# The last three steps of a tiled transformer kernel written in another order

## The reference

```
x = x + fake_quant(layernorm(x)) @ fake_quant(ctx)     # ctx: 1024 x 1024 for each sequence
x = x + attention(layernorm(x))                        # 32 heads of 32, one k and v for all, causal, alibi, @ Wo
x = x + (xf * in_scale @ sign(W).T) * out_scale + bias # xf = layernorm(x); scales = softmax(router) @ tables
```

## Time and profile before

| | |
|---|---|
| timed runs | 408.24, 407.40, 408.12 us; median 408.12 |
| profiled execution | 407.38 us, of which the profile's span is 405.6 |
| PE busy over the span | 89% |
| DVE, ACT, POOL busy over the span | 77%, 63%, 33% |
| mean granted clock of PE | 0.982 of full (2.4 GHz) |

### The profile page before, as it was taken

How to read it: one execution, slowest core, us unless ns; L and a number is a source line. 1 busy time by engine, 2 the same in 40 slices (tenths; PEclk the granted TensorE clock), 3 DMA queues, 4 the chain that set the end, 5 groups by cost and what they waited for, 6 DMA issues and landing times.

```text
span 405.6 us, 10034 instructions
## 1 busy us (share of the span) xinstructions
PE 362.7 (89%) x4162; PEld 233.9 (58%) x4162; DVE 312.1 (77%) x592; ACT 253.8 (63%) x306; POOL 133.5 (33%) x148
## 2 busy tenths in 40 slices
PE   0438977999789999999999999999999999999996
PEld 0113943874444874578557855696559655974444
DVE  6888798999846788679876997589858975496353
ACT  3857985867787877783887388648865741334021
POOL 5320043426321226312541246124612371026041
PEclk9957999999999999999999999999999999999999
DMA  7999999399999499857867587748665000100002
GB/s 303 410 373 408 409 405 391 114 322 412 311 367 347 190 288 404 302 178 196 298 229 240 147 269 263 228 153 294 225 244 131 10 2 6 50 2 0 2 1 105
DMA packets 30243, 91.56 MB, mean 226 GB/s; under 512 B 8112, under 2 KB 8496, under 8 KB 30192
## 3 DMA queue, kind: packets, MB, share of 16 engines
q1 hardware_dynamic: 28320, 84.42, 58.5%
q10 hardware_dynamic: 1872, 6.40, 4.2%
HBM read 85.05 MB, written 4.19 MB: 220 GB/s over the span
## 4 chain that ended last, share of the span: by engine, by line
PE 60%; DVE 15%; DMA 9%; ACT 7%; SPq 4%; issue 3%; POOL 0%; DVEq 0%; ACTq 0%; POOLq 0%
DMA ring<-ctx 9%; PE R L1603 9%; PE T L1426 6%; PE R L1371 5%; PE R L1372 5%; PE R L1373 5%; PE C L1407 4%; ACT b L583 4%; PE R L1462 4%; PE R L1465 3%; PE R L1464 3%; PE T L1507 3%; SPq L371 2%; PE R L1491 2%; PE R L1378 1%
## 5 line engine op out<-in xcount | busy, mean ns | idle before, releaser
L583 ACT ACTIVATE b<-ring,quant,qpar 128x2048 uint8<-128x2048 f32 x61 | 126.4, 2093 | 14.3 <-DMA ring<-ctx 8.2
L1462 PE MATMUL R<-T_hi,Wqkv_hi 128*128 128x128 f16 x448 | 77.9, 220 | 0.0
L1465 PE MATMUL R<-T_hi,Wqkv_lo 128*128 128x128 f16 x448 | 77.7, 219 | 0.0
L1464 PE MATMUL R<-T_lo,Wqkv_hi 128*128 128x128 f16 x448 | 77.7, 219 | 0.0
L1407 PE MATMUL C<-b,aT 128*64 128x512 f16 x256 | 35.7, 411 | 12.9 <-ACT b L583 6.3
L485 POOL TENSOR_TENSOR Pr<-Pr,mx 128x512 f32<-128x512 f32 x32 | 35.4, 1118 | 30.5 <-DVE mx L1069 30.5
L334 POOL TENSOR_TENSOR Pr<-Pr,mx 128x512 f32<-128x512 f32 x20 | 20.7, 1044 | 74.7 <-DVE mx L1063 74.7
L1462 PEld LDWEIGHTS R<-T_hi,Wqkv_hi 128*128 128x128 f16 x448 | 43.9, 98 | 2.0
L1464 PEld LDWEIGHTS R<-T_lo,Wqkv_hi 128*128 128x128 f16 x448 | 43.9, 98 | 0.2
L1465 PEld LDWEIGHTS R<-T_hi,Wqkv_lo 128*128 128x128 f16 x448 | 43.8, 98 | 0.0
L1371 PE MATMUL R<-Wo,attT_hi 128*128 128x512 f16 x112 | 42.5, 379 | 0.6 <-DVE attT_lo L1081 0.5
(11 more groups left out here) (172 smaller groups left out, 845.4 us busy)
## 6 DMA issues: line engine op xcount, KB each, us to landing
ring<-ctx SPq DMA_DIRECT2D x64, 1024.0 KB, 7.7
ring<-L_attn_Wo SPq DMA_DIRECT2D x4, 1024.0 KB, 9.3
ring<-L_ffn_weight SPq DMA_DIRECT2D x4, 1024.0 KB, 5.2
Wo<-L_attn_Wqkv SPq DMA_DIRECT2D x7, 544.0 KB, 15.2
X<-x ACTq DMA_DIRECT2D x6, 512.0 KB, 4.6
out<-X ACTq DMA_DIRECT2D x6, 512.0 KB, 6.2
X<-x SPq DMA_DIRECT2D x2, 512.0 KB, 11.5
sgn<-L_attn_Wqkv SPq DMA_DIRECT2D x1, 544.0 KB, 18.0
```

Of the source, the lines that this page charges most:

```text
L583: e.activation(b8[:, c % BRING, :], ring[:, slot, :], ACT.Identity, scale=qR2, bias=qZ2).then_inc(s_rf[slot], 1)
L1462: e.matmul(dst, hi, rows[0], start=k == 0 and g == 0, stop=False, skip_group_check=True)
L1464: e.matmul(dst, hi, rows[1], start=False, stop=False, skip_group_check=True)
L1465: last = e.matmul(dst, lo, rows[0], start=False, stop=k == KT - 1, skip_group_check=True)
```

## The change

`opening` is no longer called for step 7, nor `tail` for steps 8 and 9; one function `closing(s, last, end)` with Step(7), Step(8), Step(9) holds what the three did, and `burst` is called up to step 6. In it, with m = 6 and t = 7:

- PE: the context product of tile 7 is finished and its T1 and kv, query and scores come before the projection of tile 6; T1 stands between the two halves of tile 5's second FFN product, before PT of tile 6's second head half. The projection of tile 6 lies around the scores and PT of tile 7; T2 and router of tile 6 lie between the pieces of tile 7's projection. The FFN of tile 6 comes behind it: 16 matmuls ahead of tile 7's T2, 8 between T2 and the router, 8 between router and router transpose. `keep_clock(15)` and `keep_clock(6)` go; the 2 and 3 stay.
- DVE: x1(7) comes ahead of the second row sum of tile 6, norm1 right behind O's low part; the softmax of tile 7 and tile 6's x2, norm2 and router chain are put in the new order.
- POOL: the three softmax operations of tile 6, then inv_std(1, 7), then bias and sums of tile 5; with_bias(7) comes ahead of both sums of tile 6.
- Banks: projection of tile 6 goes to C, outscale of tile 6 to R 2:4, the second scores of tile 7 to R 2:4 (before R 0:2). The T banks' uses are listed in the new order. Some waits are replaced by those that the new banks ask for.

The core of the diff (PE's program, the T banks and POOL's):

```diff
+    m, t = TILES - 2, TILES - 1
+    uses += of(m, "PT00 PT01 O0") + of(t, "T10 T11") + of(m, "PT10 PT11") + of(t, "Tk") + of(m, "O1")
+    uses += of(t, "PT00 PT01 O0 PT10 PT11") + of(m, "T20 T21") + of(t, "O1")
+    uses += of(m, "rl rT is0 is1") + of(t, "T20 T21 rl rT is0 is1")
...
+            def closing(s, last, end):          # POOL
+                m, t = s.i - 1, s.i
+                subtract_max(e, m, 1, 1)
+                normalize(m, 1, 0)
+                normalize(m, 1, 1)
+                inv_std(1, t)
+                with_bias(m - 1)
+                total(m - 1, 0)
+                total(m - 1, 1)
...
+            def closing(s, last, end):          # DVE
+                m, t = s.i - 1, s.i
+                row_sum(m, 1, 0)
+                pt_lo(s, 0, 0)
+                pt_lo(s, 0, 1)
+                x1(s)
+                row_sum(m, 1, 1)
+                o_lo(s, 0)
+                norm1(s)
+                result(s, 0)
+                t1_lo(s, 0)
+                t1_lo(s, 1)
...
+            def closing(s, last, end):          # PE
+                context(s.i, 2)
+                ffn(s, 0, low)
+                pt(s, 0, 0)
+                pt(s, 0, 1)
+                context(s.i, 3)
+                ffn(s, 0, high)
+                outscale(s, 0)
+                outscale(s, 1)
+                pv(s, 0)
+                ffn(s, 1, low)
+                t1(s)
+                ffn(s, 1, high)
+                pt(s, 1, 0)
+                pt(s, 1, 1)
+                kv(s)
+                query(s, 0, low[:2])
+                tk(s)
+                query(s, 0, low[2:])
+                pv(s, 1)
+                query(s, 0, high)
+                query(s, 1, low[:2])
+                scores(s, 0)
+                query(s, 1, low[2:])
+                query(s, 1, high)
+                project(s, 0, low)
+                scores(s, 1)
+                project(s, 1, low)
+                pt(last, 0, 0)
+                pt(last, 0, 1)
+                project(s, 0, high)
+                pv(last, 0)
+                project(s, 1, high)
+                pt(last, 1, 0)
+                pt(last, 1, 1)
+                project(last, 0, low)
+                t2(s)
+                project(last, 1, low[:2])
+                pv(last, 1)
+                project(last, 1, low[2:])
+                router(s)
+                project(last, 0, high)
+                router_t(s)
+                project(last, 1, high[:1])
+                inscale(s, 0)
+                inscale(s, 1)
+                outscale(last, 0)
+                outscale(last, 1)
+                project(last, 1, high[1:])
+                ffn(last, 0, low)
+                ffn(last, 0, high)
+                t2(last)
+                ffn(last, 1, low)
+                router(last)
+                ffn(last, 1, high)
+                router_t(last)
+                keep_clock(2)
...
-                keep_clock(15)
...
-                keep_clock(6)
```

More of the change, by code:

```diff
@@ L99, in turns @@
     uses += of(0, "T20 T21 rl rT is0 is1")
-    for i in range(2, TILES + 1):
+    for i in range(2, TILES - 1):
         if i > 2:
             uses += of(i - 1, "PT00 PT01 O0 PT10 PT11 O1")
-        uses += of(i, "T10 T11 Tk") if i < TILES else []
-        uses += of(i - 1, "T20 T21 rl rT is0 is1")
+        uses += of(i, "T10 T11 Tk") + of(i - 1, "T20 T21 rl rT is0 is1")
+    m, t = TILES - 2, TILES - 1
+    uses += of(m, "PT00 PT01 O0") + of(t, "T10 T11") + of(m, "PT10 PT11") + of(t, "Tk") + of(m, "O1")
+    uses += of(t, "PT00 PT01 O0 PT10 PT11") + of(m, "T20 T21") + of(t, "O1")
+    uses += of(m, "rl rT is0 is1") + of(t, "T20 T21 rl rT is0 is1")
     return {use: n for n, use in enumerate(uses)}
@@ L119, in link, with run_steps @@
         self.e.wait_ge(self.sem, self.n)
-def run_steps(entry, step_0, step_1, opening, burst, tail):
+def run_steps(entry, step_0, step_1, opening, burst, closing):
     entry()
@@ L127, in run_steps @@
     burst(Step(2))
-    for i in range(3, TILES):
+    for i in range(3, TILES - 1):
         opening(Step(i))
         burst(Step(i))
-    tail(Step(TILES), Step(TILES + 1))
+    closing(Step(TILES - 1), Step(TILES), Step(TILES + 1))
 def at_least(e, sem, value):
@@ L327, in scores_to @@
         def scores_to(t, h):
-            return R[:, 2:4, :] if t < 2 and h == 1 else R[:, 0:2, :]
+            return R[:, 2:4, :] if t in (0, 1, TILES - 1) and h == 1 else R[:, 0:2, :]
         def subtract_max(e, t, h, b):
@@ L343, in project_to @@
         def project_to(m, n):
+            if m == TILES - 2:
+                return C[:, n, :]
             return C[:, 1 - n, :] if m == 0 else R[:, n, :]
@@ L353, in ffn_to, with outscale_to @@
             return C[:, n, :] if t == TILES - 2 else R[:, 2 + n, :]
+        def outscale_to(t):
+            return R[:, 2:4, :] if t == TILES - 2 else R[:, 0:2, :]
         last_sums = (R[:, 2, :], C[:, 0, 0:HALF // 2], C[:, 1, 0:HALF // 2])
@@ L543, in burst @@
                 normalize(s.i, 0, 1)
-            def tail(s, last):
-                t = TILES - 1
+            def closing(s, last, end):
[7 more added lines that the diff above has]
+                total(m - 1, 1)
+                subtract_max(e, t, 0, 1)
+                normalize(t, 0, 0)
+                normalize(t, 0, 1)
                 subtract_max(e, t, 1, 1)
@@ L549, in tail @@
                 normalize(t, 1, 1)
-                with_bias(t - 1)
-                total(t - 1, 0)
+                inv_std(2, m)
+                with_bias(m)
                 inv_std(2, t)
                 with_bias(t)
-                total(t - 1, 1)
+                total(m, 0)
+                total(m, 1)
                 x_t = X[t % XBUFS]
@@ L559, in tail @@
                     e.tensor_tensor(x_t[:, cols], x_t[:, cols], XL[:, cols], ALU.add).then_inc(s_y, 1)
-            run_steps(entry, step_0, step_1, opening, burst, tail)
+            run_steps(entry, step_0, step_1, opening, burst, closing)
         @block.scalar
@@ L612, in outscale_copy @@
                     e.wait_ge(s_y, t * 2)
-                e.activation(XL[:, :], R[:, 0:2, :].rearrange("p a n -> p (a n)"), ACT.Identity)\
+                e.activation(XL[:, :], outscale_to(t).rearrange("p a n -> p (a n)"), ACT.Identity)\
                     .then_inc(s_ose, 1)
@@ L858, in burst @@
                     conv(s.i + 1, 6)
-            def tail(s, last):
-                t = TILES - 1
-                exp(t, 1, 0)
+            def closing(s, last, end):
+                m, t = s.i - 1, s.i
+                conv(t, 7)
+                exp(m, 1, 0)
                 pt_hi(s, 0, 0)
                 pt_hi(s, 0, 1)
-                exp(t, 1, 1)
+                exp(m, 1, 1)
+                o_hi(s, 0)
                 outscale_copy(s)
-                o_hi(s, 0)
+                t1_hi(s, 0)
+                t1_hi(s, 1)
                 pt_hi(s, 1, 0)
                 pt_hi(s, 1, 1)
+                k_copy(s)
+                v_copy(s)
+                k_hi(s)
                 o_hi(s, 1)
+                q_hi(s, 0)
+                store(s)
+                exp(t, 0, 0)
+                exp(t, 0, 1)
+                q_hi(s, 1)
+                exp(t, 1, 0)
+                pt_hi(last, 0, 0)
+                pt_hi(last, 0, 1)
+                exp(t, 1, 1)
+                o_hi(last, 0)
+                pt_hi(last, 1, 0)
+                pt_hi(last, 1, 1)
                 t2_copy(s, 0)
                 t2_copy(s, 1)
+                o_hi(last, 1)
                 router_exp(s)
                 rt_copy(s)
+                xs_hi(s, 0)
+                xs_hi(s, 1)
+                outscale_copy(last)
+                t2_copy(last, 0)
+                t2_copy(last, 1)
+                router_exp(last)
+                rt_copy(last)
                 e.wait_ge(s_ffn, t * 2)
@@ L878, in tail @@
                     hi_part(XS[0][:, rows, :], ln2T[:, rows, :], 1.0, s_xshi)
-                outscale_copy(last)
-            run_steps(entry, step_0, step_1, opening, burst, tail)
+                outscale_copy(end)
+            run_steps(entry, step_0, step_1, opening, burst, closing)
         @block.vector
@@ L1313, in burst @@
                 softmax_in(s.i, 1)
-            def tail(s, last):
-                t = TILES - 1
-                row_sum(t, 1, 0)
+            def closing(s, last, end):
+                m, t = s.i - 1, s.i
+                row_sum(m, 1, 0)
                 pt_lo(s, 0, 0)
                 pt_lo(s, 0, 1)
-                row_sum(t, 1, 1)
+                x1(s)
+                row_sum(m, 1, 1)
                 o_lo(s, 0)
+                norm1(s)
                 result(s, 0)
+                t1_lo(s, 0)
+                t1_lo(s, 1)
                 pt_lo(s, 1, 0)
                 pt_lo(s, 1, 1)
+                result(s, 1)
+                v_lo(s)
+                k_lo(s)
                 o_lo(s, 1)
+                q_lo(s, 0)
+                scores_in(t, 0, 0)
```

(63 more changed lines are left out.)

8 lines of the change are left out of this document (removed).

## The result

The changed kernel is slower by 0.3%: median 409.29 us of 20 runs against 408.01 of 20, ratio 1.0029 with a 95% interval of 1.0017 to 1.0042. The profiled execution took 409.3 us with a span of 407.5. The time is inside the range given, but the forecast (0.2 us gained) is wrong in its sign: 1.3 us in the median and 1.9 in the profiled executions are lost, and the interval excludes no change. One run of each kernel (481.9 and 922.0 us) was slow and stays out of the ratio.

A forecast was written before the change was run, and what follows sets the result against it. TensorE's program order was taken as the bound: 9.5 us of slack less 6.75 of new waits gives 2.7 gained, less 2.5 by the clock is 0.2. Forecast 407.9 us against 408.12, range 404.6 to 410.5.

The forecast's parts named there:

- 62.0 of work: PE's real work in the rewritten stretch, priced mostly start to start from the old profile: 62.0 us of its 71.52.
- Other waits that I find by walking the new order: Smaller PE waits at scores, T2 of tile 6 and last T2, plus 0.4 before the router transpose: together 1.55 us.
- What would show it: Signs of being right: T1 wait about 5 us, slow norm1, half clock, then no PE waits over 0.5, end 12.8.
- The other small waits: PE waits at tile 7's scores, T2 of tile 6, last T2 and router transpose, summed to 1.55 us.
- The wait at T1: PE waits 5.2 us ahead of tile 7's T1: 3.2 for the norm1 chain, 2.0 from GpSimd's bias holding the port.
- even sharing: Alternative to an exclusive DVE and GpSimd port lock: norm1 would lose only some 0.8 us beside GpSimd's bias operation.
- The clock: Granted clock falls to half after T1's wait, costing 2.5 us, with bounds of 0 to 4.5.
- The 9.5 us of slack: Old stretch's time without work, 4.5 of clock-keeping matmuls and 5.0 of waits: all that the change can win.
- The last stage: From the last tile's router transpose to the span's end: taken as unchanged at 12.8 us.
- The slow rival: Clock stays low through T1, FFN, PT, kv and first queries, 9 us: 409.9 us; chance 0.2.
- The net of 0.2: Whole kernel: 2.7 us gained in the stretch less 2.5 lost by the clock gives 0.2 gained.
- The chances given: Below 407.3 us 0.43, above 408.9 0.25, within 0.32; about 0.8 us can be told from no change.

The follow-up runs named there:

- e1_o1: Changed kernel, but the second call of the last tile's projection on its low half no longer waits until O1 is emptied: 407.05 us against 407.85 before.
- e2_port: Changed kernel, but GpSimd waits for norm1 of the last tile before adding the bias of tile 5: 406.76 us against 407.85 before the change.
- e6_rowsum: Changed kernel, but tile 6's last row sum comes ahead of x1 again on DVE: 407.68 us against 407.98 before the change.
- e5_fill: Changed kernel without the low-half O1 wait, GpSimd's bias after norm1, two FFN matmuls and tile 6's low projection half ahead of T1: 402.29 us against 407.98 before.
- e3_clock: Changed kernel with 21 clock-keeping matmuls in PE's wait ahead of the last tile's T1: 406.91 us against 407.85 before the change.
- e8_two: Changed kernel without the O1 wait at the low half and with GpSimd's bias after norm1, no filler matmuls: 404.86 us against 407.98 before.
- e7_before_idle: Kernel before the change without the tail's 15 and 6 clock-keeping matmuls: 410.38 us against 407.98 with them.

## Why the prediction was wrong

The forecast for the stretch was 62.0 of work + 5.2 at T1 + 1.55 of small waits + 2.5 by the clock = 71.25 us; measured 73.44. The 2.19 between them are, rounded, 1.5 (a wait left out) + 0.9 (small waits) + 0.2 (clock) - 0.4 (T1's wait).

- **The step that failed** is "Other waits that I find by walking the new order". It missed the wait for O1 at the projection's low half, 1.5 us in the trace and 1.7 us by e1_o1. The sum of 1.55 has no term for O1, though "What would show it" promised a PE without waits of over 0.5 behind T1; at the high half of the projection, where O1 is really needed, e1_o1 shows no wait. The missed wait could be read in the code: a rule of two cases, and a call that the old order never made. With it the forecast would have been 409.4, against 409.3 measured; how close that comes is in part luck, since the other misses leave 0.7 in the trace.
- **The other small waits** were sized at 1.55 and are 2.4, 0.9 too little. The largest single one, at T2 of tile 6, had its forecast size (0.6 with the wait for its second bank). Read by starts, the five waits that were foreseen come to about 1.55 in the trace. The rest lies in seams of about 0.1 between kinds of matmul, at scores and PV for instance, which prices taken from start to start within one kind don't hold; it was not separated by a run. The old order had such seams too: the profile marks only 1.9 us of waits in its stretch, where the forecast counted 5.0 and took all of it as time that could be won.
- **The wait at T1** was right in place, cause and size: 335.60 against a forecast of 335.7. PE came to it 0.3 later than forecast, so the wait is 4.8 and not 5.2. Each part of it was confirmed by a run: the port (e2_port), and normalize on the path (e6_rowsum). Norm1's length of 2.75 was forecast as about 2.9. The Trainium skill, page "SBUF — State Buffer", section "SBUF: two separate sides", has the shared port pair held for the whole instruction. The trace agrees, 2.75 against 0.81 without the collision. One reading ahead of it was weak: the 1.54 of the earlier trace rows doesn't speak against even sharing, by which it would have been up to 1.6; only the 2.98 does.
- **The clock** was right: it fell, and took 2.7 against 2.5.
- **The 9.5 us of slack** in the old order could never be won whole, by the seams above; with the added waits mended (e5_fill) 5.5 came out of it in the trace, 5.6 by time. **The last stage** stayed at 12.8.
- **The slow rival** named the right side and nearly the right time (409.9) by a mechanism that didn't happen: the clock was low for 5.5 us of work, not 9.

The net of 0.2 was a difference of two large terms, 9.5 and 9.3, so one missed wait of 1.5 decided its sign. The chances given (0.25 for slower) held that poorly: most unseen waits could only be on the slow side, since all work was counted and any wait not found adds.

## What to carry to other kernels

When work is put in another order by hand, go through each helper's waits for the arguments of its new calls, not only for those that the old order made. Before a wait is added on a chain through DVE and GpSimd, look at what GpSimd has next: here a GpSimd operation of 2.34 us that began 0.14 earlier held back a DVE norm of 0.80, both from SBUF to SBUF, until 2.75 were gone, and one semaphore behind the norm gave it back. Where TensorE must wait for 3 us, fill the wait with real work whose bank is free, or with matmuls that nobody reads (2.1 us here, e3_clock).

## What the runs showed of the hardware

A tensor_scalar of 128x1024 from SBUF to SBUF that began up to 0.14 us behind a GpSimd operation ended 0.55 us after that operation's end (0.54 in one) in five traces (before, changed kernel, e1_o1, e3_clock, e6_rowsum), whether that operation was 1.04 or 2.34 long. Alone it takes 0.80; why 0.55 are enough behind the other isn't shown. The granted clock fell to half in PE waits of 4.6 and 3.6 us (the changed kernel and e1_o1, e6_rowsum), in a wait of 2.7 or 0.3 us behind one (e2_port, e8_two), and 0.3 us behind one of 3.1 (e7_before_idle), by the profile's brackets and each time after dense work. After the 2.7 it was back sooner than after the 4.6: 1.6 and 1.7 us of work lost in e2_port and e8_two, 2.7 in the changed kernel. The scatter of 2 to 3 us between runs stays where the clock is kept in the stretch (e3_clock); its source was not found.
